# Two cross-attention layers on one core: the last steps of each layer reordered in pieces

## The reference, cut to what matters

```python
q      = x @ Wq                                  # (8, 100, 640)
text   = softmax(q_h @ k_h.T  * scale) @ v_h     # k, v = text @ Wk, text @ Wv, per head
ip     = softmax(q_h @ kip_h.T * scale [+ 0.5 * sem]) @ vip_h
out    = (text + ip [* spatial_mask]) @ Wo + bo + x   # x of the next layer
```

## Time and profile before

| | us |
|---|---|
| median of three runs | 1839.28 |
| the profiled execution | 1835.73 |
| its span, first to last instruction | 1833.9 |
| PE busy | 1763.1 (96%) |
| DVE busy | 1208.7 (66%) |
| ACT busy | 777.4 (42%) |
| POOL busy | 429.2 (23%) |

### The profile page before, as it was taken

How to read it: one execution, slowest core, us unless ns; L and a number is a source line. 1 busy time by engine, 2 the same in 40 slices (tenths; PEclk the granted TensorE clock), 3 DMA queues, 4 the chain that set the end, 5 groups by cost and what they waited for, 6 DMA issues and landing times. The chain is left out here.

```text
span 1833.9 us, 52042 instructions
## 1 busy us (share of the span) xinstructions
PE 1763.1 (96%) x22067; PEld 1420.8 (77%) x22067; DVE 1208.7 (66%) x2967; ACT 777.4 (42%) x1569; POOL 429.2 (23%) x520
## 2 busy tenths in 40 slices
PE   7988999999999999998999899999999999999998
PEld 4667888888888888885566688888888888888884
DVE  5775676767676767554654376767676767676673
ACT  3243554545545455453222243434444435344351
POOL 3031423334242433321100011211121212122120
PEclk9999999999999999999999999999999999999999
DMA  6742443434334344334146322414142324223221
GB/s 255 159 168 75 137 146 114 148 94 142 107 130 135 109 128 123 114 121 172 58 37 176 109 68 52 124 43 132 51 118 65 105 64 118 58 86 97 79 64 45
DMA packets 123583, 198.36 MB, mean 108 GB/s; under 512 B 41704, under 2 KB 110712, under 8 KB 116760
## 3 DMA queue, kind: packets, MB, share of 16 engines
q1 hardware_dynamic: 117880, 164.50, 31.4%
q10 hardware_dynamic: 5472, 30.54, 4.7%
HBM read 133.91 MB, written 60.88 MB: 106 GB/s over the span
## 5 line engine op out<-in xcount | busy, mean ns | idle before, releaser
L513 PE MATMUL proj<-w_hl,cbuf 128*128 128x128 f16 x9600 | 601.1, 219 | 0.7 <-issue 0.7
L513 PE MATMUL proj<-cbuf,w_hl 128*128 128x322 f16 (+1 forms) x3840 | 591.5, 300 | 2.7 <-issue 2.2
L513 PEld LDWEIGHTS proj<-w_hl,cbuf 128*128 128x128 f16 x9600 | 548.5, 98 | 2.8 <-issue 1.0
L513 PEld LDWEIGHTS proj<-cbuf,w_hl 128*128 128x128 f16 x3840 | 367.4, 97 | 166.5 <-issue 2.8
L1252 POOL TENSOR_TENSOR arena<-arena 128x400 f16<-128x400 f32 x240 | 235.9, 983 | 893.1 <-ACT arena L1011 893.1
L1010 ACT ACTIVATE arena<-st,rs 128x400 f16<-128x400 f32 x480 | 287.2, 598 | 285.3 <-DVE st L1634 167.7
L986 ACT ACTIVATE arena<-proj 128x323 f16<-128x323 f32 (+1 forms) x160 | 70.7, 442 | 516.5 <-PE proj L513 503.3
L1011 ACT ACTIVATE arena<-st,rs 128x400 f32<-128x400 f32 x480 | 285.8, 595 | 0.0
L1553 DVE TENSOR_TENSOR arena<-arena 128x400 f16<-128x400 f32 x240 | 144.9, 604 | 134.8 <-ACT arena L1011 131.7
L662 PE MATMUL pv<-arena 128*128 128x34 f16 (+3 forms) x3840 | 191.9, 189 | 6.9 <-POOL arena L1252 5.7
L662 PEld LDWEIGHTS pv<-arena 128*128 128x128 f16 x3840 | 173.5, 97 | 30.3 <-POOL arena L1252 9.4
(11 more groups left out here) (156 smaller groups left out, 1651.2 us busy)
## 6 DMA issues: line engine op xcount, KB each, us to landing
arena<-k_dram SPq DMA_DIRECT2D x240, 185.2 KB, 3.6
k_dram<-arena SPq DMA_DIRECT2D x160, 161.2 KB, 1.9
c_dram<-cbuf SPq DMA_DIRECT2D x16, 1290.0 KB, 6.4
raw<-ctx_dram SPq DMA_DIRECT2D x14, 1290.0 KB, 7.9
cbuf<-c_dram SPq DMA_DIRECT2D x12, 1290.0 KB
cbuf<-w_dram ACTq DMA_DIRECT2D x24, 640.0 KB, 7.3
arena<-q_dram SPq DMA_DIRECT2D x48, 125.0 KB, 2.6
cbuf<-c_dram ACTq DMA_DIRECT2D x2, 2580.0 KB
```

What stands on the lines that cost most here:

```text
L513: mm = nc.tensor.matmul(out, x[a](k), w[b](k), start=(k == 0 and m == 0), stop=(k == KT - 1 and m == 2))
```

## The change

On PE, output products are cut into pieces of one to four k (a k is one 128-row slice of the contraction) and laid between the maxima of the last step but one, and between score tiles and PVs in the last step (`last_window`). The first four k of the next product (`q_tile(1, 0, 0)`, or `out_tile(1, 1, 0)` at the end) come into the last step too. `out_tile(l, 0, 0)` waits for bank A's `v_unit` only, and `out_tile(l, 0, 1)` for bank B's. The waits of `q_tile(1, half, 0)` for the output tiles are made k by k. DVE's and ACT's orders follow; `split_weight(1, 0)` on ACT is made in two parts between the q tiles 2, 3 and 4, and the loads of weight 2 come after them.

```diff
-            def linear(weight, src, *name, ks=range(CT)):
+            def linear(weight, src, *name, ks=range(CT), each_k=None):
                 for k in ks:
+                    if each_k:
+                        each_k(k)
                     mm = nc.tensor.matmul(bank[:, 0:MT], weight[:, c, k], src[:, k],
...
-                if c == 0:
-                    if l:
-                        for t in range(CT):
-                            bank_done(pe, "out", 0, half, t)
-                    else:
-                        pe.wait_ge(x_in[half], 16)
-                linear(wq, xq[l][half], "q", l, half, c)
+                linear(wq, xq[l][half], "q", l, half, c, ks=ks,
+                       each_k=(lambda k: bank_done(pe, "out", 0, half, k)) if l and c == 0 else None)
...
-                if c == 0:
+                if c < 2:
                     row_done(pe, "oT", (l + 1) * STEPS - CT + ks[-1] - (0 if half else STEPS // 2))
                     if half == 0:
                         pe.wait_ge(wo_in, 16 * (l + 1))
-                        pe.wait_ge(v_low, 2 * (l + 1) * STEPS)
+                if half == 0 and c < 2:
+                    pe.wait_ge(v_low, 2 * (l + 1) * STEPS - 1 + c)
...
+            def last_window(l, u):
+                def next_product(first, last):
+                    if l:
+                        out_tile(l, 1, 0, range(first, last))
+                    else:
+                        q_tile(1, 0, 0, range(first, last))
+                out_tile(l, 0, 2, range(2))
+                score_tile(u, 0)
+                out_tile(l, 0, 2, range(2, 3))
+                score_tile(u, 1)
+                out_tile(l, 0, 2, range(3, CT))
+                score_tile(u, 2)
+                out_tile(l, 0, 3, range(2))
+                score_tile(u, 3)
+                o_turn(u - 1)
+                out_tile(l, 0, 3, range(2, 4))
+                weigh(u, 0)
+                score_tile(u, 4)
+                out_tile(l, 0, 3, range(4, CT)), out_tile(l, 0, 4, range(1))
+                weigh(u, 1)
+                score_tile(u, 5)
+                out_tile(l, 0, 4, range(1, 3))
+                weigh(u, 2)
+                out_tile(l, 0, 4, range(3, CT))
+                weigh(u, 3)
+                next_product(0, 2)
+                weigh(u, 4)
+                next_product(2, 4)
+                weigh(u, 5)
...
 # PE, the last step but one (more2 is false)
                 max_scores(n, 0)
-                    out_tile(l, 0, 0)
+                    out_tile(l, 0, 0, range(2))
                 weigh(u, 3)
                 max_scores(n, 1)
+                    out_tile(l, 0, 0, range(2, 4))
                 weigh(u, 4)
                 max_scores(n, 2)
-                    out_tile(l, 0, 1)
+                    out_tile(l, 0, 0, range(4, CT)), out_tile(l, 0, 1, range(2))
                 weigh(u, 5)
                 max_scores(n, 3)
+                    out_tile(l, 0, 1, range(2, CT))
                 max_turn(n)
...
 # PE, between the layers
-            q_tile(1, 0, 0)
+            q_tile(1, 0, 0, range(4, CT))
+            q_tile(1, 0, 1)
             o_turn(STEPS - 1)
-            q_tile(1, 0, 1)
+            q_tile(1, 0, 2)
             weight_turn(1, 0)
-            for c in range(2, CT):
+            for c in range(3, CT):
                 q_tile(1, 0, c)
...
 # PE, after layer 2
-            out_tile(1, 1, 0, range(CT - 1))
+            out_tile(1, 1, 1, range(4))
             o_turn(2 * STEPS - 1)
-            out_tile(1, 1, 0, range(CT - 1, CT))
-            for c in range(1, CT):
+            out_tile(1, 1, 0, range(4, CT)), out_tile(1, 1, 1, range(4, CT))
+            for c in range(2, CT):
                 out_tile(1, 1, c)
...
 # ACT, between the layers
-            q_tile(1, 0, 0)
+            q_tile(1, 0, 0), q_tile(1, 0, 1)
             o_turn(STEPS - 1)
-            q_tile(1, 0, 1)
-            row_filled(act, "oT", STEPS - 1)
-            split_weight(1, 0)
+            q_tile(1, 0, 2)
+            split_weight(1, 0, (0, 1))
+            q_tile(1, 0, 3)
+            split_weight(1, 0, (2, 3))
+            q_tile(1, 0, 4)
             load_weight(1, 2)
-            for c in range(2, CT):
-                q_tile(1, 0, c)
             split_weight(1, 1)
...
 # DVE: out_tile(l, 0, c) is read out
 #   0: after maxima(n, 2) instead of before it
 #   1: after shift_put(u) of the last step instead of before it
 #   2: before add_semantic(u, 2) instead of after prob_low(u, 2)
 #   3: between add_semantic(u, 4) and (u, 5) instead of after prob_low(u, 4)
 #   4: after prob_low(u, 4) in both layers (in layer 2 it stood after normalise)
```

## The result

The changed kernel takes 1824.36 us (median of 4 runs, 1824.0 to 1827.54) against 1840.09 for the one before beside it; the ratio of the runs is 0.9928, 95% interval 0.9909 to 0.9948, so 13 us (10 to 17) less. Predicted were 11.8 us less, 1827.5, in 1823.5 to 1834, so the median lies 0.9 inside the lower end of the range. In a second timing (experiment 8) the ratio is 0.9930 (0.9913 to 0.9946), 1826.65 beside 1838.4.

What follows compares the result with a forecast made beforehand. PE was taken as the bound, busy 1763.1 of 1833.9 us, so only its idle time could be gained. Gains of 6.9 (first layer) and 4.9 (second) sum to 11.8, taking 1839.28 to 1827.5; range 1823.5 to 1834.

Steps and rivals of the forecast that it cites:

- wait before head 1, layers 1 and 2: Last step but one: PE arrives before DVE ends head 0's maximum, new waits of 0.7 and 1.4 us.
- last PV of layer 1 earlier by: End of layer 1: six waits removed, four k of q tile 0 moved ahead; last PV starts 4.7 us earlier, at 865.7.
- turn of weight 0 earlier by: Between the layers: from this turn on DVE's chain is 5.75 us earlier, 4.7 + 1.05.
- wait before output tile (0, 1, 2): Between the layers: PE needs a bank that DVE's fixed order reads out late; new wait of 3.9 us.
- that tile earlier by: Output tile (0, 1, 2) between the layers: gain 8.2 us, not the 12 that the removed waits suggest.
- layer 2's end: Second layer's last two steps: 6.9 of waits less 1.4 before head 1 and 0.6 for pieces, gain 4.9 us.
- text stage: Behind the first layer: taken as moved whole, no change of its own; a rival (0.13) had the layer's gain given back there.
- first rival: Between the layers: the clock holds through the new wait; gain 13.5 us, 1825.8; chance 0.15.
- Pieces: Last two steps of each layer: nine more piece entries at 0.07 us each, 0.6 per layer; bounds 0 and 0.26 each.
- slower case: Fourth rival: entering fp32 pieces costs far more; loses from 0.72 us each, at 0.9 gives 1842.5; chance 0.05.
- clock term: Behind the new wait of 3.9 us: one fall of the granted clock, 5.12 against 3.4, charged 1.7 us.
- its second: First q tiles behind layer 1's PVs: the earlier clock fall comes all the same; gain 10.1 us, 1829.2; chance 0.12.

Runs made afterwards that it cites:

- experiment 8: Kernel before profiled twice more and changed kernel timed and profiled again, both unaltered, to study the text stage; changed against before 0.9930, 1826.65 beside 1838.4 us.
- Experiments 1 and 4: Both against the changed kernel: 1, ACT splits weight 0 of layer 2 whole, 0.9955 to before; 4, DVE reads two output tiles out earlier, 0.9901 to before.
- experiment 3: Changed kernel with five more fp32 matmul pairs, result unread, in PE's wait before output tile (0, 1, 2); ratio to before 0.9929, stretch from M1 1.70 us shorter.

## Why the prediction was right

By its own steps, from M1 in the first profiles of both kernels:

| step | predicted | measured |
|---|---|---|
| wait before head 1, layers 1 and 2 | 0.7, 1.4 | 0.71, 1.34 |
| waits in the last steps | none | none |
| last PV of layer 1 earlier by | 4.7 | 4.81 |
| turn of weight 0 earlier by | 5.75 | 5.86 |
| wait before output tile (0, 1, 2) | 3.9 | 3.77 |
| that tile earlier by | 8.2 | 8.25 |
| clock behind that wait | 1.7 | 1.7, then 3.0 |
| ACT's wait at q tile (1, 1, 2) | 0.36 | 0.41 |
| first text product earlier by | 6.9 | 6.85 |
| layer 2's end | 4.9 | 4.6 |
| text stage | 0 | 2.9, within its own spread |

- The number was held with some luck. 1824.36 is below the 1825 to 1831 that the forecast had for itself, and closer to the first rival's 1825.8 (the clock holds); yet the clock fell, as forecast. The stretches gave 11.5 us, and the rest is the text stage's. The table's agreement within 0.3 is also that of the first two profiles. Over all pairs of profiles the first text product is earlier by 4.6 to 7.6 us and layer 2's end by 4.6 to 6.4, as the clock falls or not. What does not depend on the pair are the waits and arrivals: 0.7 and 1.3 before head 1 (0.65 and 1.34 in the second profile), none in the last steps, 3.77 before the output tile.
- The step that carried it was to follow DVE's order behind the removed waits, not to add the waits up. The wait of 2.77 for ACT and 4.7 us of earlier PVs would have given 12 in layer 1; 8.2 was left, since DVE's two 5.7 us blocks on weights stood ahead of the read-outs. Experiments 1 and 4 show both halves: with ACT's long wait back only a few us are lost, and with DVE's order altered 6 are gained.
- Pieces cost what was charged: two k take 1.41 from start to start (853.04 to 854.45 above), 0.07 over 1.34. The slower case, 0.72 a piece, had nothing in it.
- The clock term was right by size in the first profile (experiment 3: 1.70), but not all of its reasoning. I took the fall of the earlier trace rows for a cost that before always pays. It doesn't: the second and third profiles of before have the same PVs and waits and a full clock behind them, and the third falls behind 2.22 and 2.77 instead. PE's timeline of the third profile:

```profile
891.62 5.32 PE L479 MATMUL proj<-extra,cbuf 128*128 128x400 f32 x10 [2.77 <-ACT qo L936]
...
1789.67 5.29 PE L479 MATMUL proj<-qo,cbuf 128*128 128x400 f32 x10 [2.22 <-DVE arena L1518]
```

  In both of these profiles the tile behind the PVs takes 3.60 at a granted clock of 1.00 (5.29 in the first). The sum was hardly touched, as 1.05 of late turn was all that it had in it, and before's second profile is shorter by just that, 86.2. The rule of the Trainium skill (TensorE: Matmul & The Clock Gate, "Loop structure matters more than you think"), that a read-out doesn't cool the engine where the next matmuls follow at once, agrees with two of before's three profiles: these PVs don't always cool the engine. It doesn't cover the one in which they did. The prediction's rival on this point is its second (its text says third): the same fall, in the changed kernel. It didn't come in either profile, with the turn of weight 0 at 33.40 and 33.35 after M1.
- The text stage was assumed to move whole. The averages, 114.6 for before and 113.7 for the changed kernel, differ by 1.0, but an assumption of exactly nothing should have had its bounds: the stage varies by 4.5 us in before alone, more than most terms of the sum. The 13 us of the ratio lie between the 11.5 of the stretches and the 14.3 with the text stage's luck.

## What to carry to other kernels

When a wait is removed on the bounding engine, go down the written order of each other engine to the next thing that the bounding one needs from it, and compare arrivals; the gain is the smaller of the two. A read-out of 0.6 us that frees a bank should not stand behind 8 us of work that nobody waits for yet. And a wait of nearly 4 us on PE costs more than its length here: filling it with useless products was 1.7 us faster in that stretch.

## What the runs showed of the hardware that was not expected

The granted clock fell behind waits of 2.2 and 2.8 us in some executions and not in others of the same kernel. The same is seen at one product of the text stage that no kernel changed. Behind a wait of 2.50 it took 8.35 us in the changed kernel's second profile (the first line, from PE's timeline) and 6.68 in the third of before (the second line):

```profile
1009.98 8.35 PE L513 MATMUL proj<-w_hl,t_hl 128*128 128x320 f16 x48 [2.50 <-issue]
```
```profile
1015.82 6.68 PE L513 MATMUL proj<-w_hl,t_hl 128*128 128x320 f16 x48 [2.50 <-issue]
```

Before's second profile kept the granted clock at 1.00 there even behind 3.19. Behind the wait of 3.77 it fell in all six profiles that have it, and three output tiles took 12.0 to 13.3 us instead of 10.3, so 1.7 to 3.0 us a time.

The stretch T to M2, 39 steps of layer 2 that no kernel changed, was 740.7 to 740.8 in eight profiles and 742.0 to 743.5 in the other six. The clock tells them apart: in each of the six the granted clock was 0.50 for at least 2 us within the first 4 us behind T, after two waits of 1.5 us for the maxima, and in the eight it was 1.00 throughout that place. From T to the next step's turn it is 18.2 us in the eight and 19.4 to 20.9 in the six. PE's timelines of the first and then of the third profile of before show the same 24 matmuls just behind T:

```profile
1043.89 1.50 PE L513 MATMUL proj<-w_hl,cbuf 128*128 128x128 f16 x24
```
```profile
1043.55 2.73 PE L513 MATMUL proj<-w_hl,cbuf 128*128 128x128 f16 x24
```

So here the clock fell behind two waits of 1.5 us, 2 us apart, in some executions. What decides in which ones, no run here says.
